# One block for scores, weights and messages of a graph layer, with operands of the messages in PSUM

## What is computed

```python
# layer 0
scores = leaky_relu(e_s[src] + e_d[dst], 0.2)                  # (E, 4)
m = segment_max(scores, dst); ex = exp(scores - m[dst])
denom = segment_sum(ex, dst)
agg = segment_sum((ex / denom[dst])[:, :, None] * h[src], dst)  # (N, 4, 64)
# layer 1: the same with s[src] + s[dst], 8 heads of 32, and loops
out = segment_sum(Vh[src] * a[:, :, None], dst)
```

## Time and profile before

| | us |
|---|---|
| median of 3 runs | 3146.72 (3133.33 to 3147.36) |
| the profiled execution | 3144.7 |
| its span | 3142.8 |
| scores, weights, messages of layer 0 (first to last instruction of DVE) | about 107 to 488, 488 to 554, 554 to 1202 |
| the same of layer 1 | about 1607 to 2148, 2148 to 2287, 2287 to 2817 |

### The profile page before, as it was taken

How to read it: one execution, slowest core, us unless ns; L and a number is a source line. 1 busy time by engine, 2 the same in 40 slices (tenths; PEclk the granted TensorE clock), 3 DMA queues, 4 the chain that set the end, 5 groups by cost and what they waited for, 6 DMA issues and landing times. The chain is left out here.

```text
span 3142.8 us, 35335 instructions
## 1 busy us (share of the span) xinstructions
PE 1798.8 (57%) x10362; PEld 1444.4 (46%) x10362; DVE 1769.9 (56%) x2713; ACT 368.8 (12%) x715; POOL 1701.8 (54%) x1504
## 2 busy tenths in 40 slices
PE   2301292777755553999741112693177777756668
PEld 2200182555544442799740000693155555535557
DVE  6200098867644447455730000699787777757756
ACT  1100001000000001445200000000300000004244
POOL 3577606887877775000047777205878788761010
PEclk8655596888877776899865555797588888878889
DMA  3355553455433332000135566433145554430000
GB/s 121 119 190 189 173 184 95 126 160 162 136 92 92 92 91 74 1 1 0 63 89 196 196 200 198 148 117 112 54 146 165 162 165 162 134 115 8 4 31 34
DMA packets 140778, 361.01 MB, mean 115 GB/s; under 512 B 39352, under 2 KB 65360, under 8 KB 126890
## 3 DMA queue, kind: packets, MB, share of 16 engines
q0 software_dynamic: 69760, 225.91, 24.0%
q1 hardware_dynamic: 65866, 122.18, 11.2%
q10 hardware_dynamic: 5088, 12.13, 1.1%
HBM read 289.00 MB, written 71.12 MB: 115 GB/s over the span
## 5 line engine op out<-in xcount | busy, mean ns | idle before, releaser
L756 POOL DMA_INDIRECT e_ring<-table,e_index x840 | 1101.4, 1311 | 369.7 <-issue 255.5
L1121 PE MATMUL ms_ps_m<-ms_msg,ms_pick 128*128 128x260 f32 (+1 forms) x2816 | 830.4, 461 | 373.0 <-issue 258.2
L1121 PEld LDWEIGHTS ms_ps_m<-ms_msg,ms_pick 128*128 128x128 f32 x2816 | 634.4, 230 | 568.8 <-issue 432.3
L657 PE MATMUL sc_ps_e<-sc_keys,sc_hot 125*128 125x100 bf16 (+1 forms) x3840 | 353.7, 240 | 569.5 <-issue 561.3
L620 DVE TENSOR_REDUCE all_xn<-sc_ps_e 128x800 f32 (+1 forms) x240 | 234.1, 1019 | 633.7 <-remote 527.8
L657 PEld LDWEIGHTS sc_ps_e<-sc_keys,sc_hot 125*128 125x128 bf16 x3840 | 272.7, 102 | 650.3 <-issue 633.3
L795 POOL DMA_INDIRECT all_acc<-table,e_stage_index x416 | 397.1, 955 | 142.4 <-issue 141.1
L1098 DVE TENSOR_TENSOR ms_msg<-e_ring,all_xn 128x1040 f32 x176 | 218.0, 1239 | 254.1 <-SPq L1063 135.6
L1098 DVE TENSOR_TENSOR ms_msg<-e_ring,e_weight 128x1056 f32 x176 | 220.9, 1255 | 128.1 <-SPq L1063 112.7
L1094 DVE SCALAR_TENSOR_TENSOR ms_pick<-graph_dst_col,graph_tile_base,graph_lane_row 128x512 f32<-128x512 f32 x352 | 263.7, 749 | 12.0 <-issue 9.8
L1107 DVE TENSOR_TENSOR all_acc<-all_acc,ms_ps_m 128x260 f32 (+1 forms) x352 | 150.3, 427 | 8.3 <-PE ms_ps_m L1121 8.0
(11 more groups left out here) (415 smaller groups left out, 2682.0 us busy)
## 6 DMA issues: line engine op xcount, KB each, us to landing
ahead<-all_acc POOLq DMA_DIRECT2D x32, 1056.0 KB
e_ring<-ahead SPq DMA_DIRECT2D x32, 1056.0 KB
sc_rows<-src_low SPq DMA_DIRECT2D x160, 200.0 KB
ahead<-all_acc POOLq DMA_DIRECT2D x20, 1040.0 KB
e_ring<-ahead SPq DMA_DIRECT2D x20, 1040.0 KB
e_ring<-table,e_index POOLq DMA_INDIRECT x840
sc_rows<-src_high ACTq DMA_DIRECT2D x160, 50.0 KB
all_acc<-table,e_stage_index POOLq DMA_INDIRECT x416
```

Of the source, the lines that this page charges most:

```text
L657: mm = pe.matmul(ps_e[lane][:, t * SLOT:t * SLOT + C], hot[0:KEYS, q, cols], keys[0:KEYS, part, :, :].rearrange("p g h -> p (g h)"), start ...
L756: pool.indirect_dma_start(out=g.ring[:, slot * QUAD + i // GT, i % GT, :], out_offset=None, in_=s.table[:, :], in_offset=bass.IndirectOffs ...
L1121: mm = pe.matmul(ps_m[b][:, 0:W], pick[:, b, t, :], msg[:, b, t, :], start=t == 0, stop=t == GT - 1)
```

## The change

Each graph layer is one block now, without barriers inside; semaphores `picked`, `back_copied` and `stored` stand for what the barriers ordered.

- The stage of `gather_ahead` lies in the last four groups' room of the ring and no more in `acc`.
- POOL gathers all 8 quads of the ring after the last score is picked (`picked`), and none inside the scores part; before the last two of them it waits for the stage to be stored.
- Before the messages DVE alone zeroes `acc`, after the last copy of the weights (`back_copied`); ACT copies the row 0..127 (`lane_row`) to PSUM, and in layer 0 all weights too. In layer 1 ACT copies each step's weights to one of three banks.
- DVE's order in a step is pick, add, msg. The sums use two banks.

```diff
 def edge_weights(...)
+        @block.gpsimd
+        def _(pool):
+            pool.wait_ge(between.picked, picks)
+            for q in range(RQ):
+                if q == RQ - 2:
+                    pool.wait_ge(stage.stored, 16 * stage.order.ahead)
+                gather_quad(pool, s, g, 0, q, QUAD)
...
 def pass_messages(...)
-        ps_m = [m.ps(f"ps_m{i}", [P, 512]) for i in range(DEPTH)]
+        BANKS = 2
+        ps_m = [m.ps(f"ps_m{i}", [P, 512]) for i in range(BANKS)]
+        ps_lane = m.ps("ps_lane", [P, 512])
+        lane_row = ps_lane[:, 0:P]
+        ps_w = m.ps("ps_w", [P, ET, H]) if most is None else [m.ps(f"ps_w{i}", [P, 512]) for i in range(DEPTH)]
...
+        @block.scalar
...
+                act.activation(ps_w[b][:, 0:GT * H].rearrange("p (t h) -> p t h", h=H), weight[:, bass.ds(group * GT, GT), :], ACT.Copy).then_inc(weight_set, 1)
+                act.activation(msg[:, b, :, R:W], most[:, bass.ds(group * GT, GT), :], ACT.Copy).then_inc(tail_ready, 1)
+
+            act.wait_ge(between.back_copied, backs)
+            act.activation(lane_row, s.lane_row[:, :], ACT.Copy).then_inc(near_set, 1)
+            if most is None:
+                act.activation(ps_w[:, :, :], weight[:, :, :], ACT.Copy).then_inc(weight_set, 1)
...
+            dve.wait_ge(between.back_copied, backs)
+            dve.memset(acc[:, :, :], 0.0).then_inc(acc_zero, 1)
...
-                pool.memset(acc[:, NT // 2:NT, :], 0.0).then_inc(acc_zero, 1)
...
-                    if later(fixed, DEPTH):
-                        pe.wait_ge(added, n - (DEPTH - 1))
+                if later(fixed, BANKS):
+                    pe.wait_ge(added, n - (BANKS - 1))
...
 def edge_layer(...)
-        early = 3 if room >= 2 else 0
-        filled = RQ - 1 if room >= 2 else RQ
...
-        stage = Stage(s, e, "sc" + layer, order, acc[:, :, :].rearrange("p a w -> p (a w)"), D + H)
+        stage = Stage(s, e, "sc" + layer, order, g.ring, D + H)
...
+        with nc.Block() as block:
+            picks = edge_scores(nc, s, block, between, stage, "sc" + layer, edge, parts, node, s.dst_scores[int(layer)], s.lines[int(layer)],
+                                dst_line, dst_start, H)
+            backs = edge_weights(nc, s, block, between, g, stage, picks, "wt" + layer, edge, dst_line, dst_start, acc, weight, H, self_loops)
+            pass_messages(nc, s, block, between, g, stage, backs, "ms" + layer, weight, most, acc, H, loads)
```

More of the change, by code:

```diff
@@ new lines, in _, with load @@
+        @block.sync
+        def _(sp):
+            def load(it, q, first):
+                if not first:
+                    sp.wait_ge(hot_ready, it - lanes + 1)
+                sp.dma_start(rows[0:LOW, q, :], s.src_low[bass.ds(it * (ITEM * P), ITEM * P)].partition_broadcast(LOW)).then_inc(row_in[q], 16)
+            for q in range(lanes):
+                load(q, q, True)
+            with steps_of(sp, lanes, NITEM, lanes) as it0:
+                for q in range(lanes):
+                    load(it0 + q, q, False)
@@ L809, in gather_ahead, with edge_weights @@
     store(stage.order.ahead - 1, (stage.order.ahead - 1) % 2)
-def edge_weights(nc, s, g, early, filled, tag, edge, dst_line, dst_start, acc, best_weight, H, self_loops):
+def edge_weights(nc, s, block, between, g, stage, picks, tag, edge, dst_line, dst_start, acc, best_weight, H, self_loops):
     GH = 4
@@ L971, in pass_messages @@
+        return CT * len(backs)
+def pass_messages(nc, s, block, between, g, stage, backs, tag, weight, most, acc, H, loads=()):
     O = D // H
@@ new lines, in _, with free, gather, report @@
+        @block.gpsimd
+        def _(pool):
+            def free(quad):
+                pool.wait_ge(msg_ready, freed(ENG.Pool, quad))
+            def gather(turn, slot, groups):
+                if not order.is_ahead(turn, slot):
+                    gather_quad(pool, s, g, turn, slot, groups, free)
+            quads(pool, gather)
+        @block.sync
+        def _(sp):
+            if loads:
+                sp.wait_ge(between.back_copied, backs)
+            for dst, src in loads:
+                sp.dma_start(dst, src).then_inc(loaded, 16)
+            sp.wait_ge(stage.stored, 16 * stage.order.ahead)
+            lead = min(3, order.spacing - 1)
+            def report(turn, slot, groups):
+                if slot + lead < RQ and order.is_ahead(turn, slot + lead):
+                    i, first = order.ahead_index(turn, slot + lead), (slot + lead) * QUAD
+                    sp.wait_ge(msg_ready, freed(ENG.SP, turn * RQ + (slot + lead)))
+                    sp.dma_start(ring[:, first:first + QUAD, :, :].rearrange("p a t f -> p (a t f)"),
+                                 s.ahead[bass.ds(i, 1), :, 0:QUAD * GT * (D + H)].rearrange("a p f -> p (a f)")).then_inc(ahead_in, 16)
+                if order.is_ahead(turn, slot):
+                    sp.wait_ge(ahead_in, (order.ahead_index(turn, slot) + 1) * 16)
+                else:
+                    sp.wait_ge(row_in[slot % SETS], order.before(turn, slot, True) * (16 * QUAD * GT) + 16 * groups * GT)
+                sp.sem_inc(rows_landed, groups)
+            for slot in range(RQ):
+                report(0, slot, QUAD)
+            quads(sp, report)
+            if loads:
+                sp.wait_ge(loaded, 16 * len(loads))
```

542 lines of the change are left out of this document (249 added, 293 removed).

## The result

The changed kernel took **3287.82 us** (median of 4 runs, 3280.14 to 3288.90), the kernel before 3144.61 us in the same comparison: a ratio of **1.0457**, 95% interval 1.0427 to 1.0488. The forecast was 2902 us, 386 us less. It was wrong in sign.

A forecast was written before the change was run, and what follows sets the result against it. GpSimd's gathers were taken to bound both messages parts. Layer 0's -127, layer 1's -132 and +14 us gave -245 from 3144.7, so 2900, plus 2 us for the median: 2902 us; 8-in-10 range 2870 to 2968.

The forecast's parts named there:

- (a): Messages parts: with operands in PSUM, msg and pick no longer hold gathers; -121 us in layer 0, -125 in layer 1.
- (b): Layer 0: without 24 early gathers the scores end 30 us sooner, but those gathers follow later, +30 us; together nil.
- (c): Before the messages: barriers and GpSimd's zeroing go; -6 us in layer 0, -7 us in layer 1.
- (d): Messages steps: the order pick, add, msg with two banks costs or gains nil.
- (e): Copies of weights on ScalarE in both layers: nil; uncovered, some 2 us a layer.
- (g): Loads of quads gathered ahead: 1 MB needs about 4 us and must land within 10 us; nil.
- (f): Start of the messages, eight steps ahead of the loop: TensorE slowed beside faster gathers; +14 us, bounds 0 and +30.
- The third: Rival: TensorE starves in the messages loop too with gathers 1.25 us apart; half of 246 us lost, 3025 us; chance 7%.
- First: Rival: the pick still holds gathers through its scalar in SBUF; 64 us, giving 2966 us; chance 7%.
- second: Rival: nothing is freed, as any long VectorE instruction holds gathers; 3134 us; chance 5%.
- fourth rival: VectorE reads the PSUM operands at half speed in the messages; +124 us, 3271 us, slower than before; chance 3%.

The follow-up runs named there:

- prompt comparisons: Those where the kernel before took 2935 to 2937 us; the changed kernel took 2660.69 us against 2935.39 us there, ratio 0.9065.
- late comparisons: Those where the kernel before took 3133 to 3145 us; the changed kernel took 3287.82 us against 3144.61 us there, ratio 1.0457.

## Why the prediction was wrong

**(a) Operands in PSUM: the mechanism was right.** The gathers went to 0.95 us, msg and pick held at 1239 and 741 ns, and VectorE paid nothing for PSUM. In the prompt comparisons the two operands are worth 2893.05 - 2660.69 = 232 us; the sum said 246. The Trainium skill (SBUF — State Buffer, "Who interferes with whom") infers that a tensor_tensor with both inputs in SBUF doesn't stall descriptor generation. The measurement is otherwise: with the msg's weights back in SBUF a gather takes 1217 ns in the mean, without 947. With the pick's row back, which is no tensor_tensor, it is 990.

**(b) Early gathers, (c) barriers.** The scores of layer 0 ended at 457.5 us, 29 earlier (30 forecast), and the first pick stood at 527.1 (525 forecast). In layer 1 the stretch from the last reduce to the first pick went from 140.5 to 133.7 us, the 7 us of (c). But the reading behind (b) was too narrow. I saw TensorE nearly stop beside the 24 early gathers and took the rest of the scores for sound. The same question asked of the 160 gathers ahead would have shown 270.4 us of "remote" ahead of VectorE's reduces, in the trace that I had.

**(d) Order and banks, (e) copies, (g) loads.** The old order gave 2661.25 against 2660.69 us prompt and lost as much late: nil, as said. Copies and loads had no run of their own; in the late trace the msg waits 0.6 us in all, so neither was on the path there. The working of (g) has a slip: 1 MB at 433 GB/s is 2.5 us, not 4, and in the prompt trace of the kernel before such a load lands 5.0 us after its issue.

**(f) Start of the messages: here the sum failed**, at +14 us, bounds 0 and +30. The messages took 753 and 599 us where the forecast had 551 (525 to 1076) and 405: these 202 and 194 us are more than the whole miss of 386. By the runs, operands in PSUM with what follows from them were worth +144 us in the late comparisons (+143 against -1), where (a) and (f) said -232. The step that misled me is in (f): "In the loop of the messages it does not: from 860 to 1200 us there are 564 passes beside 238 gathers." Those passes ran while msg held the gathers to one in 2.15 us (the 238 are 231 gathers and 7 copies of indices), and gathers ran 1.25 us apart only while VectorE and TensorE waited for rows. The row showed TensorE beside *held* gathers, and I used it for free ones. The contention that the change removes was what kept TensorE's completions in time. The row that bears on free ones was at hand: the earlier trace rows have gathers at exactly the distance that the change brings, and a wait of 25.44 us in one burst; I kept it for the first eight steps.

**The rivals.** The third, that TensorE starves in the loop too, is what happened, at 7% and with half its price: it lost "half of the 246", where more than all went. I stopped at half because I took the full ring for a brake that restores the old pace. It isn't one: at the old pace a gather came every 2.15 us with TensorE's completions in time, while now the engines take turns in bursts, and GpSimd stands 355 us. First, second and fourth rival are out: gathers don't end 0.82 us after a pick, and msg is not over 1.24 us. The price of the first was high: with the pick's row in SBUF it measured 41 us, not 64.

**The chances.** In a prompt comparison the forecast of 2902 us would have been missed as well, by 241 us, since the kernel before starts 208 us lower there; the difference, -245, would have been near the -275 measured. Nothing in a single trace of the kernel before said that this trace was of one of two kinds.

**What the other 43 us are.** Prompt, the changed kernel with both operands in SBUF (`sbuf_both`) gains 43 us where (c) said 13: without lateness the scores end at 262 us, and in the kernel before the barrier then held the first pick until 478.7 us, behind GpSimd's gathers; without the barrier the first pick is at 328.8 us.

## What to carry to other kernels

Before a wait or a contention is removed, ask who profits from it now: here VectorE's hold on GpSimd spaced the gathers, and in the late comparisons TensorE needed the spaces. A row shows an engine beside others *at their present pace*; for a faster pace only a stretch that has that pace is evidence, however short. And where a queue of small DMAs is freed from one brake, have a cheap one ready: fills that widen each gather's distance by 0.16 us turned +4.6% into -8.1% in the late comparisons.

## What the runs showed of the hardware

- In late comparisons TensorE's completions, and in the scores its matmuls too, come late beside indirect gathers that GpSimd issues 1.25 us apart (adds wait 578.5 us), less at 1.32 us (307.6), not to be told from the prompt kind at 1.41 us (102.8 against 102.3; the scores still wait 319.3), and not at 1.81 us (no wait above 1.9 us in layer 0's messages). In the messages of the changed kernel waits of 5 to 20 us end some 3 us after the last gather of a burst, or inside it. In prompt comparisons the same instructions at 1.25 us wait 53.2 us in all. What differs between the occasions, and by what path gathers reach TensorE, stays open; the lateness is in the timed runs as in the profiled ones, and the ring's gathers (950 and 947 ns in the messages of layer 0) and msg (1239 ns) take the same time in both. No more code is loaded either: in the kernel before each of the two instruction queues moves 32 packets in both kinds.
- The page SBUF — State Buffer of the Trainium skill ("Who interferes with whom") gives TensorE ports of its own and lets DMAs contend with no engine. If so, what delays it is not a port of SBUF; no run here shows whether it is.
- A fill of one element on GpSimd has 116 ns in its row, but eight behind each other take 0.31 us, with 0.15 us left to the next gather where the gap without fills is 0.30: eight fills widen 1.25 us to 1.41, one of 700 elements (0.70 us) to 1.81.
- In the starved scores of the kernel before, TensorE's granted clock was 0.50, the lower of its levels, from 200 to 350 us, with 70 passes in 150 us. In the changed kernel's (late) the starved matmuls come singly and evenly: from 201.37 to 229.37 us eleven of them, 0.24 us each, 2.79 to 2.81 us from start to start.
